# 30 result buffers, the extra tile's list made early, and row sums that begin in accumulating DMAs

## The reference

```
xn   = layernorm(x)
out  = x + retention(xn) + moe(xn)

retention: 8 heads of 32, decay g per head; q, k, v = xn @ W + b; causal inside each batch,
           carried from chunk to chunk in a state S (d x d per head)
moe:       scores = softmax(xn @ gate.T) over 64 experts; the best 6 with renormalised weights
           per expert e: (silu(xn @ g_e) * (xn @ u_e) * weight) @ down_e, 176 hidden columns
           plus two shared experts (352 hidden columns) for every token
```

## Time and profile before

| | |
|---|---|
| time, median of 3 runs | 279.58 us (279.53 to 282.41) |
| profiled execution, its time | 281.07 us |
| profiled execution, its span | 279.3 us |
| busy: PE / DVE / ACT / POOL | 90% / 70% / 59% / 65% of the span |

### The profile page before, as it was taken

One profiled execution on the slowest core, in us unless ns is written; L12 is line 12 of the kernel. 1 busy time (PEld: TensorE's weight loads), 2 busy tenths in 40 slices (PEclk: granted clock), 3 DMA queues, 4 the chain that ended last, 5 costly groups with the idle time before them and its releaser, 6 DMA issues.

```text
span 279.3 us, 6132 instructions
## 1 busy us (share of the span) xinstructions
PE 251.3 (90%) x1586; PEld 213.8 (77%) x1586; DVE 196.1 (70%) x530; ACT 165.6 (59%) x468; POOL 180.5 (65%) x156
## 2 busy tenths in 40 slices
PE   8887878699999999999999999865989999999971
PEld 6653666499999999999999889764974446899971
DVE  3859937677877777877778777745754636559995
ACT  1378506588778888888888777455744546414300
POOL 5196636756777878788787877777377787303121
PEclk9999979999999999999999999998999999799995
DMA  7999622899898979988888898989212122399711
GB/s 218 299 376 337 225 56 62 274 302 289 287 273 289 279 254 289 306 266 266 273 289 288 293 281 270 310 275 364 100 44 79 56 72 70 80 390 419 270 40 39
DMA packets 27770, 64.58 MB, mean 231 GB/s; under 512 B 6068, under 2 KB 13468, under 8 KB 27744
## 3 DMA queue, kind: packets, MB, share of 16 engines
q1 hardware_dynamic: 20080, 47.88, 51.4%
q0 software_dynamic: 7664, 16.41, 18.5%
HBM read 58.53 MB, written 11.01 MB: 249 GB/s over the span
## 4 chain that ended last, share of the span: by engine, by line
PE 56%; DVE 18%; DMA 9%; issue 7%; POOL 4%; ACT 3%; SPq 0%; POOLq 0%; DVEq 0%; ACTq 0%
PE ps L1210 16%; PE ps L1238 8%; PE ps L1239 8%; PE ps L1308 7%; DMA digits<-table,gcol 5%; PE ps L1196 4%; PE ps L1220 4%; POOL digits L471 4%; DVE act_slab L1027 2%; DMA parts<-tab_slab,scol 2%; DVE one_hots L780 2%; DVE pT L1050 2%; PE ps L1361 2%; DVE act_slab L1030 2%; DMA x_slab<-in_x 1%
## 5 line engine op out<-in xcount | busy, mean ns | idle before, releaser
L471 POOL DMA_INDIRECT digits<-table,gcol x65 | 76.5, 1177 | 30.8 <-issue 15.3
L1210 PE MATMUL ps<-w_split,xT_both 128*128 128x352 f32 x390 | 86.7, 357 | 6.7 <-ACT xT_both L575 6.6
L1210 PEld LDWEIGHTS ps<-w_split,xT_both 128*128 128x128 f32 x390 | 66.5, 190 | 12.5 <-issue 8.0
L833 DVE TENSOR_TENSOR w_split<-w_ring,w_split 128x704 fp32r<-128x704 f32 x65 | 57.5, 885 | 1.1 <-ACT w_split L569 0.5
L569 ACT CAST w_split<-w_ring 128x704 fp32r<-128x704 f32 x65 | 51.0, 785 | 0.0
L825 DVE SCALAR_TENSOR_TENSOR act_slab<-ps,digits,sg 128x176 f32<-128x176 f32 x64 | 25.6, 400 | 33.7 <-ACT sg L581 29.0
L487 POOL DMA_INDIRECT parts<-tab_slab,scol x33 | 37.3, 1129 | 10.1 <-issue 8.9
L1238 PE MATMUL ps<-w_ring,act_slab 128*128 128x256 f32 x130 | 39.4, 385 | 0.0
L1239 PE MATMUL ps<-w_slab,act_slab 128*128 128x256 f32 x130 | 39.1, 383 | 0.0
L838 DVE TENSOR_TENSOR xT_both<-ps,xT_both 128x256 fp32r<-128x256 f32 x65 | 27.1, 416 | 3.6 <-ACT xT_both L575 3.6
L1196 PE MATMUL ps<-k,digits 128*128 128x128 f32 x130 | 25.4, 277 | 4.5 <-DMA digits<-table,gcol 3.8
(11 more groups left out here) (174 smaller groups left out, 413.1 us busy)
## 6 DMA issues: line engine op xcount, KB each, us to landing
w_ring<-in_w SPq DMA_DIRECT2D x65, 480.0 KB, 3.8
w_slab<-in_w SPq DMA_DIRECT2D x65, 48.0 KB, 4.9
w_split<-parts SPq DMA_DIRECT2D x4, 768.0 KB, 7.6
early_w<-parts SPq DMA_DIRECT2D x2, 768.0 KB, 7.3
digits<-table,gcol POOLq DMA_INDIRECT x65, 5.2
x_slab<-in_x SPq DMA_DIRECT2D x4, 256.0 KB, 3.6
table<-tab_slab POOLq DMA_DIRECT2D x1, 1024.0 KB, 8.3
tab_slab<-in_x SPq DMA_DIRECT2D x2, 512.0 KB, 6.3
```

The source lines that it names most:

```text
L471: pool.indirect_dma_start(out=rows[:, r, :], out_offset=None, in_=table, in_offset=bass.IndirectOffsetOnAxis(ap=gcol[:, r:r + 1], axis=0), ...
L833: V.tensor_tensor(rr(w_lo[:, k % 2, :]), w1_sb[:, k % RING, 0:4 * F], w_hi[:, k % 4, :], ALU.subtract).then_inc(wlo_sb, 1)
L1210: ins = mm(ps[2 + k % 2][:, 0:2 * F], rr(a[:, k % 2, h * P:(h + 1) * P]), rr(b[:, k % (2 if b is w_lo else 4), h * 2 * F:(h + 1) * 2 * F]) ...
```

## The change

- Result buffers: 30 instead of 24, in another order; six of them lie in `route`, where the extra tile's selection (two buffers) and the retention's states (four) live at other times. DVE waits for these buffers' scatters: for two of them before the loop over further tiles, for four before it clears the states.
- The extra tile: the pieces stand at tiles 6 to 11, the list is read at tile 53, and POOL gathers the tile as number 64 in the ordinary order, before scatter 33 instead of after scatter 38. POOL's special order at tiles 56 to 59 is gone. Additions of the k and v biases stand at tiles 16, 20, ... 44. DVE's loop is written out.
- Sums: SP loads only the first three rows, for two chunks at a time (four loads of 384 KB, into four places, with no reuse). POOL adds the other three rows onto them by four accumulating DMAs. DVE sums pairs of chunks in three adds of 512 columns. Chunks 0 and 1 are summed after the decay of chunk 4, and so on; POOL's and DVE's final adds wait for the pair.
- Preparation: DVE makes the high digits first; ACT converts the low digits, not DVE.
- Semaphores are merged (`shared_in` to 96, `columns_ready`, `zero_ready`, `kT_sb`, `out_done`, `waited`).

```diff
-Y_BUFS = 24
+Y_BUFS = 30
-        y_bufs = [early_w[:, b * H:(b + 1) * H] for b in range(y_early)]
-        y_bufs += [tab_slab[:, b * H:(b + 1) * H] for b in range(y_table)]
...
+        y_bufs = blocks(early_w, 0, 5) + blocks(product_slab, 0, 4) + blocks(route, 0, 2)
+        y_bufs += blocks(route, 6 * H, 2) + blocks(early_w, 5 * H, 1) + blocks(route, 2 * H, 2)
+        y_bufs += blocks(tab_slab, 0, NC * ROW // H) + blocks(end_of_hots, 0, 3)
+        Y_PRODUCTS, Y_STATES, Y_SELECT = range(5, 9), (9, 10, 14, 15), (14, 15)
...
-        LISTED = (8,)
+        LISTED = (4,)
...
-            def load_parts(c):
-                if c >= SUM_CHUNKS:
-                    sp.wait_ge(parts_read, c - SUM_CHUNKS + 1)
-                sp.dma_start(part_sb[c % SUM_CHUNKS], parts_v[:, c, :, :]).then_inc(parts_in[c % SUM_CHUNKS], 16)
-
-            load_parts(0)
+            for q in range(PAIRS):
+                sp.dma_start(part_sb[q], parts_v[:, 2 * q:2 * q + 2, 0:TOPK // 2, :]).then_inc(pair_in[q], 16)
             for n in range(2):
                 sp.dma_start(x_again[:, 4 * n:4 * n + 4, :], x_v[:, 4 * n:4 * n + 4, :]).then_inc(x_again_in, 16)
-            for c in range(1, SUM_CHUNKS):
-                load_parts(c)
...
-            for t in range(late):
-                if t < plain:
-                    fetch(t, t)
-                count = 1 + t % 2 if t >= plain else int(t >= SCATTER_LAG and t % 8 not in SCATTER_SKIPPED)
-                for _ in range(count):
+            for t in range(TILES - AHEAD):
+                fetch(t, t)
+                if t >= SCATTER_LAG and t % 8 not in SCATTER_SKIPPED:
                     scatter(scattered)
                     scattered += 1
-            fetch(plain, plain)
             for t in range(scattered, TILES):
                 scatter(t)
...
+            for q in range(PAIRS):
+                pool.wait_ge(pair_in[q], 32)
+                pool.dma_start(part_sb[q], parts_v[:, 2 * q:2 * q + 2, TOPK // 2:TOPK, :], accum_op=ALU.add)\
+                    .then_inc(parts_added[q], 16)
             for c in range(NC - 1):
                 pool.wait_ge(o_sb, c + 1)
-                pool.wait_ge(x_sum, c + 1)
+                pool.wait_ge(x_sum, c // 2 + 1)
...
+                    act_e.wait_ge(lo_ready, 1)
+                    nc.scalar.copy(lo_h[:], lo_i[:]).then_inc(lo_ready, 1)
...
-            V.tensor_scalar(lo_i[:], rank_i[:], 15, None, ALU.bitwise_and)
             link(V.tensor_scalar(hi_i[:], rank_i[:], 4, None, ALU.arith_shift_right))
-            V.tensor_copy(lo_h[:], lo_i[:])
             V.tensor_copy(hi_h[:], hi_i[:]).then_inc(digits_ready, 1)
+            V.tensor_scalar(lo_i[:], rank_i[:], 15, None, ALU.bitwise_and).then_inc(lo_ready, 1)
...
+            PIECES_FROM, BIAS_FROM, BIAS_EVERY = 6, 16, 4
+            for t in range(TILES):
+                if t - (E - RING) - 1 in LISTED:
+                    dve.wait_ge(y_sb, t - 1)
+                    extra_indices(0, ps[6 + t % 2])
+                expert_dve(t)
+                if 0 <= t - PIECES_FROM < len(pieces):
+                    pieces[t - PIECES_FROM](0, link)
+                if t >= BIAS_FROM and (t - BIAS_FROM) % BIAS_EVERY == 0 and (t - BIAS_FROM) // BIAS_EVERY < NC:
+                    bias_kv((t - BIAS_FROM) // BIAS_EVERY)
...
+            for b in Y_SELECT:
+                dve.wait_ge(y_out[b], y_stores(b))
...
-            def sum_parts(c):
...
+            def sum_parts(q):
+                pair = slice(2 * q, 2 * q + 2)
+                dve.wait_ge(parts_added[q], 16)
+                if q >= 1:
+                    dve.wait_ge(x_sum, q)
+                link(V.tensor_tensor(total[:], part_sb[q][:, :, 0, :], part_sb[q][:, :, 1, :], ALU.add))
+                V.tensor_tensor(total[:], total[:], part_sb[q][:, :, 2, :], ALU.add).then_inc(total_ready, 1)
+                if q == 0:
                     dve.wait_ge(x_again_in, 32)
+                dve.wait_ge(total_ready, q + 1)
+                V.tensor_tensor(x_again[:, pair, :], total[:], x_again[:, pair, :], ALU.add).then_inc(x_sum, 1)
...
-            LAST_SUMS = [[], [], [0], [1, 2], [3], [4, 5], [6], [7]]
+            LAST_SUMS = [[], [], [], [0], [1], [2], [3], []]
...
+            for b in Y_STATES:
+                dve.wait_ge(y_out[b], y_stores(b))
             V.memset(state[:], 0.0).then_inc(state_zero, 1)
```

More of the change, by code:

```diff
@@ L357, in slot_free @@
                 sp.wait_ge(y_ps, t + 1)
[L358 removed]
+                sp.sem_inc(waited, 1)
             with sp.Fori(0, E // RING - 1) as i:
@@ L373, in _ @@
             half = (C32_LATE + C32W) // 2
-            late += [(k32[:, lo:hi], c32[:, lo:hi], late_in) for lo, hi in ((C32_LATE, half), (half, C32W))]
+            late += [(k32[:, lo:hi], c32[:, lo:hi], shared_in) for lo, hi in ((C32_LATE, half), (half, C32W))]
             for n in range(RING + EXTRA):
@@ L426, in _ @@
                     sp.wait_ge(last_sb, 1)
-                sp.dma_start(out_v[:, c, :], x_again[:, c, :]).then_inc(out_done[c % 2], 16)
-            for k in range(2):
-                sp.wait_ge(out_done[k], 16 * (NC // 2))
+                sp.dma_start(out_v[:, c, :], x_again[:, c, :]).then_inc(out_done, 16)
+            sp.wait_ge(out_done, 16 * NC)
         @block.gpsimd
@@ L944, in _ @@
-            pieces_at = {0: (extra_expert, 0), 1: (extra_base, 0), 4: (extra_select, 0), 5: (extra_place, 0),
-                         6: (extra_hot, 0), 7: (extra_hot_rest, 0)}
-            for k in range(4):
-                expert_dve(k, k, first=True)
-                if k in pieces_at:
-                    piece, n = pieces_at[k]
-                    piece(n, link)
-            with dve.Fori(0, E // RING - 1) as i:
-                for k in range(4, RING + 4):
-                    expert_dve(i * RING + k, k)
-                    if k in (9, 17):
-                        bias_kv(i * 2 + (k // 17))
@@ L956, in _ @@
-            for k in range(4, RING + EXTRA):
-                if k - 1 in LISTED:
-                    dve.wait_ge(y_sb, E - RING + k - 1)
-                    extra_indices(LISTED.index(k - 1), ps[6 + (k - 2) % 2])
-                expert_dve(E - RING + k, k, last=True)
-                if k in pieces_at:
-                    piece, n = pieces_at[k]
-                    piece(n, link)
-                if k in (10, 12):
-                    bias_kv(NC - 2 + (k - 10) // 2)
+                    w_low(t + 2, t + 2)
@@ new lines, in expert_dve @@
+                if t + 1 < E:
+                    gate_up(t + 1, t + 1, rows[:, (t + 1) % AHEAD, H + t + 1:H + t + 2])
+                elif t + 1 < TILES:
+                    j = t + 1 - E
+                    dve.wait_ge(sg_sb, t + 2)
+                    extra_weight((t + 1) % AHEAD, j, link)
+                    gate_up(t + 1, t + 1, ov_s[:, 4:5])
+                if ahead:
+                    x_low(t + 2, t)
+                if t >= E:
+                    extra_dest(t % AHEAD, t - E, link)
+                    place = ov_s[:, 5:6]
+                else:
+                    place = rows16[:, t % AHEAD, 2 * (H + E) + t:2 * (H + E) + t + 1]
@@ L1067, in _ @@
                 if n == 0:
-                    for b in range(y_early + y_table, y_early + y_table + 4):
+                    for b in Y_PRODUCTS:
                         dve.wait_ge(y_out[b], y_stores(b))
```

138 lines of the change are left out of this document (47 added, 91 removed).

## The result

The changed kernel is slower. Its median is 295.23 us (291.77 to 298.54, 7 runs), that of the kernel before, run beside it, 278.66 us (276.79 to 282.41, 7 runs); the ratio is 1.052, with a 95% interval of 1.0467 to 1.0573. The forecast was 271.3 us, with a range of 267 to 277.

A forecast was written before the change was run, and what follows sets the result against it. It took late scatters and gathers behind POOL's backlog to bound the loop, DVE the last stretch. Net -3.2 us at the third unit and -5.1 for row sums made -8.3: span 271.0, median 271.3, range 267 to 277.

The forecast's parts named there:

- Preparation (-0.4): DVE's chain to the lists loses one conversion of 0.43 us; taken as -0.4 us for all that follows.
- Buffers: Loop end: 30 buffers end the scatter waits; tile 64 transposed 8.75 us earlier, shared units start at 202.3 instead of 211.43.
- The new waits on DVE: Shared units: DVE's scatter waits hold the third unit to 213.5 against 218.5; gain 4.9 us, not 9.1, net -3.2.
- The 1.7 us that I charged: PE after its stop before the third shared unit: lower clock costs 1.7 us; bounds 0 and 1.7 again in the tail.
- Row sums (-5.1): Last stretch: DVE's sums fall from about 18 to 9 us; last add at 271.1 instead of 276.25, gain 5.1 us.
- the loads and accumulating DMAs: Behind the last scatter: 3 MB in about 15 us, fourth accumulate landed by 253; charged nothing, up to 2.5 us if slow.
- The accumulates are slow: Tail rival: accumulates one after another set the end, up to 291.4 us; 0.11 for 5.4 to 8.9 us each, 0.11 slower.

The follow-up runs named there:

- early `x`: Against the changed kernel, SP loads x as soon as the eight result buffers it overwrites are scattered, ahead of its wait for the rest; 279.21 us, ratio 1.0036.
- the stop gone and the old sums: Changed kernel with the loads and sums of the kernel before, and DVE's state clearing moved behind the shared part's last product; 279.45 us, ratio 1.0009.
- plain copies: Against the changed kernel, POOL's four DMAs copy the second three rows over the first three instead of adding them; 286.15 us median.
- DVE's clearing moved and two plain chunks: Changed kernel with x loaded early, chunks 0 and 1 loaded whole without accumulating, state clearing moved behind the sixth product; 277.58 us, ratio 0.994.
- four plain chunks: Changed kernel with x loaded early, state clearing behind the sixth product, four chunks loaded whole, only pairs 2 and 3 accumulated; 278.27 us, ratio 0.9998.

## Why the prediction was wrong, point by point

**Preparation (-0.4).** About right. Where no low clock falls into the first 64 us, the first gather is issued at 41.5 to 42.0 with the new preparation and, in one execution, at 42.16 with the old one.

**Buffers.** The mechanism was right: ACT waits for no scatter from 150 to 203 us, and the shared units start at 203.83 (forecast 202.3). The size was off mostly on the other side of the subtraction: 211.43 was late, against 208.77 and 208.90 in the two other profiles of this loop. Against these the gain at this place is 5 us, not 9.1; over all profiles with 30 buffers, which start these units at 201.12 to 206.80, it is 2 to 8.

**The new waits on DVE.** The working held nearly to the digit: clearing at 210.83 (forecast 210.5), third unit at 213.59 (213.5). But with 3.51 us a unit the third began at 215.9 in the second profile of the kernel before, so the gain is 2.3 us instead of 4.9; at chunk 1's scores it is 2.2 in the kernel after (233.29 against 235.47) and 0.1 in the one with early `x` (235.34), which lost the rest at a clock of 0.79 behind the stop. The 1.7 us that I charged for that were about right for five of the seven profiles with this stop, where the third unit took 5.08 to 5.37 us; in the other two, one of them the kernel after, it took 3.67. What the sum takes for granted, that a gain here reaches the end, did not hold: with the stop gone and the old sums, 5 us at chunk 1's scores were worth nothing in time (1.0009).

**Row sums (-5.1).** Three adds of 0.69 us a pair, as forecast. The gain was read from DVE as the bound of the last stretch; the change makes DMA the bound instead. With only this repaired, early `x`, the time is that of the kernel before (1.0036).

**The step that failed: the loads and accumulating DMAs.** I charged nothing. Three things in it were wrong.
- The size: 768 KB a transfer, not 384.
- The price: about 15 us of DMA, the fourth landed by 253. By this study's rows it is four plain transfers at 1.9 us, four accumulating at 4.1 and 1 MB of `x` at 2.6 by the same plain rate, together 26.6 us. The last pair was issued at 251.30 and landed 18.5 us later, at 269.8.
- The cover: the fourth sum's turn was put at about 263, the first's some 13 us before, and at most 2.5 us were charged if the first copy was slow. But the first sum's third add also needs `x`; its bytes stood in the sum, its landing was not asked for. The change moves `x` from second to last on SP: it was issued at 242.21 and landed at 269.5, and chunk 5's decay stood behind that add on DVE. In place of nothing, this cost 16.4 us of PE standing still.

The Trainium skill (Collectives: The Full Stack, "The bandwidth ceiling") has an add in the DMA engine cost a second source read and nothing more; that would make 2 x 1.9 = 3.8 us, and 4.1 was measured, so this rule nearly agrees.

**The rival.** "The accumulates are slow" had the right side, for a reason only half right. Its formula (last landing + 2.2 + 0.43 + 2.62) gives 275.1 from 269.8, not 293.4, because it left DVE's order out: a late first sum holds up the decays, PE stops for 16.4 us, and the three chunks left then run at a clock of 0.64.

**Why `x` came so late.** More than 22 us for 1 MB issued before any accumulating copy: it stood behind the plain loads and then moved one packet of 1 KB for each accumulating packet of 3 KB (804 against 814). The Trainium skill (DMA: Bandwidth & Descriptors, "SWDGE vs HWDGE vs iDMA") has each engine take turns between the queues that the two kinds of issue feed; the counts agree, with plain copies too (247 against 248; there `x` took 17.7 us).

**What stays open.** That `x` in larger pieces would come sooner was not tried. Also open is how long TensorE stays at 1.2 GHz in a given execution: two profiles of the kernel with DVE's clearing moved and two plain chunks have spans of 282.0 and 275.8 us, more than the edits below 1% move, and it was not controlled here. Why the first profile's loop ended late was not tested.

## What to carry to other kernels

Follow each operand of the first instruction that waits, not only the transfer that the change is about: here two DMA issues in another order were worth 14 us. An add moved from an engine into DMA is not free where the DMA engines are already full; an accumulated byte cost 2.1 times a plain one, and work whose data comes late must not stand in an in-order queue ahead of work that is ready. And take a profile's late events as one execution's: 2.5 of the 9.1 us subtracted here were its own. Where two queues share the DMA engines packet for packet, as here, a load in small pieces beside one in large pieces gets little of them.

## What was not expected of the hardware

- An accumulating copy from DRAM into SBUF occupied the DMA engines 4.1 us for 768 KB, a plain one 1.9; full engines moved 225 GB/s with it, against 385 without.
- A load issued 2.5 to 9 us before the accumulating copies, on another queue, landed at 269.5, beside the last of them (269.8): 22.5 us in the median of its two halves, against 4.7 when it was first.
- SP's queue and POOL's moved packet for packet, 804 and 814 in 14 us, though one's were 1 KB and the other's 3 KB.
- An add of 128x512 on DVE took 0.69 us alone and 1.10 us while POOL ran adds of 128x256 beside it (at 262.84 in the kernel with four plain chunks).
- After the stop of 16.4 us the granted clock was 0.64 on the mean for the last 25 us; and with PE idle for no more than 1.66 us from 201 on it was 0.50 from 236 to 244 us in one kernel and 0.99 in another.
